# Rebuilding the opening of a fused two-layer adapter kernel: softmax, activation table, fillers, mixing matrices and column sums

## What is computed

```
y0 = grouped_conv1d(x, 9 taps, 4 groups) + (cond @ c_weight.T + side)      # layer 0
x1 = x + ffn0(y0)
h  = gelu(gelu(cond @ W0 + b0) @ W1 + b1);  att = softmax(h @ W2 + b2)     # 8 kernels, per sample
y1 = einsum('boi,bih->boh', att @ kernels, x1) + att @ bias_k              # layer 1
out = x1 + ffn1(y1)

ffn(y) = y @ W_base.T + b_base + 2 * sum_e gate_e(y) * (y @ A_e.T) @ B_e.T
gate   = softmax over the two largest of 8 logits y @ W_router.T, 0 elsewhere
```

## Time and profile before

| what | us |
|---|---|
| median of 3 runs | 398.42 |
| lowest and highest | 396.69, 398.55 |
| the profiled execution | 398.19 |
| its span, first to last instruction | 396.4 |
| TensorE busy | 386.1 |
| DVE, ScalarE, GpSimd busy | 280.5, 207.4, 226.6 |

### The profile page before, as it was taken

The page is one execution under the profiler, slowest core; times in us unless marked ns, Lnnn a source line. Parts: engine busy times, 40 slices in busy tenths (PEclk is TensorE's granted clock), DMA queues, the critical chain, the costliest instruction groups (busy, mean ns, idle before and its releaser), DMA issues.

```text
span 396.4 us, 9115 instructions
## 1 busy us (share of the span) xinstructions
PE 386.1 (97%) x2789; PEld 376.2 (95%) x2789; DVE 280.5 (71%) x983; ACT 207.4 (52%) x529; POOL 226.6 (57%) x199
## 2 busy tenths in 40 slices
PE   7989999999999999999999999999999999999996
PEld 6668999999999999999999999999999999999995
DVE  2787776767667776766777676677767667776764
ACT  3847455555445555544555554455555445555541
POOL 3387765555566565556656555665655566565560
PEclk9999999999999999999999999999999999999999
DMA  7871212222221122222111222212212221121101
GB/s 248 294 157 55 79 49 62 63 73 80 80 80 51 56 66 67 80 80 80 53 54 57 75 80 80 80 53 53 65 67 80 80 80 55 51 70 63 56 27 55
DMA packets 19821, 31.04 MB, mean 78 GB/s; under 512 B 5920, under 2 KB 6208, under 8 KB 19808
## 3 DMA queue, kind: packets, MB, share of 16 engines
q1 hardware_dynamic: 19808, 30.89, 25.2%
HBM read 21.97 MB, written 8.91 MB: 78 GB/s over the span
## 4 chain that ended last, share of the span: by engine, by line
PE 90%; DVE 4%; issue 2%; DMA 1%; ACT 1%; POOL 1%; SPq 0%; DVEq 0%; ACTq 0%; POOLq 0%
PE ps_out L336 33%; PE ps_out L348 22%; PE ps_out L368 11%; PE ps_conv L304 11%; PE ps_mix L384 5%; PE ps_t L316 4%; PE ps_mix L387 2%; DMA pack<-in_pack 1%; PE ps_t L355 1%; DVE yT L632 1%; PE ps_out L355 1%; DVE wb L632 1%; POOL x1b L902 1%; DVE lb_w L648 0%; PE ps_out L395 0%
## 5 line engine op out<-in xcount | busy, mean ns | idle before, releaser
L336 PE MATMUL ps_out<-wa,yT 128*128 128x392 f32 x768 | 152.4, 345 | 1.0 <-ACT yT L483 0.7
L336 PEld LDWEIGHTS ps_out<-wa,yT 128*128 128x128 f32 x768 | 132.2, 188 | 4.4 <-DVE yT L632 1.0
L889 POOL TENSOR_TENSOR x_part<-x,x_part 128x512 fp32r<-128x512 f32 x31 | 40.1, 1293 | 115.2 <-ACT x_part L483 115.2
L348 PE MATMUL ps_out<-wb,yT 128*128 128x256 f32 x768 | 104.4, 285 | 0.2 <-DVE wb L632 0.2
L348 PEld LDWEIGHTS ps_out<-wb,yT 128*128 128x128 f32 x768 | 96.0, 189 | 0.4 <-issue 0.4
L483 ACT ACTIVATE yT<-ps_t 64x256 fp32r<-64x256 f32 x128 | 48.4, 378 | 29.4 <-PE ps_t L316 26.9
L368 PE MATMUL ps_out<-lb_w,hwT 128*128 128x256 f32 x384 | 59.1, 289 | 1.1 <-issue 0.4
L632 DVE TENSOR_TENSOR yT<-ps_t,yT 64x256 fp32r<-64x256 f32 x128 | 53.8, 420 | 3.0
L902 POOL TENSOR_TENSOR x1b<-x,base_bias 128x512 f32<-128x512 f32 x30 | 39.7, 1324 | 26.4 <-DVE res L759 26.4
L520 ACT ACTIVATE wts<-top 128x1 f32<-128x1 f32 x128 | 30.3, 284 | 46.1 <-DVE top L723 46.1
L304 PE MATMUL ps_conv<-x_part,conv_w 128*128 128x256 f32 x384 | 52.1, 285 | 0.0
(11 more groups left out here) (93 smaller groups left out, 478.0 us busy)
## 6 DMA issues: line engine op xcount, KB each, us to landing
x_raw<-in_x_phase SPq DMA_DIRECT2D x32, 260.0 KB, 2.7
x_tok<-in_x_tok SPq DMA_DIRECT2D x32, 256.0 KB, 2.6
out<-res SPq DMA_DIRECT2D x31, 256.0 KB, 2.0
wa_raw<-in_wa SPq DMA_DIRECT2D x2, 784.0 KB, 8.1
wb_raw<-in_wb SPq DMA_DIRECT2D x2, 512.0 KB, 9.2
lb_raw<-in_lb SPq DMA_DIRECT2D x2, 256.0 KB, 6.1
bias<-in_bias SPq DMA_DIRECT2D x2, 256.0 KB, 6.0
scratch<-mix_nat SPq DMA_DIRECT2D x1, 512.0 KB, 2.8
```

The costliest lines, as they stand in the source:

```text
L336: last = mm(out_banks(y, t)[:, 0, 0:AR + DH], yT[y][dp][:, k, :], wa[y][:, wp, k, :], start=(n == 0 and k == 0), stop=(n == len(SPLITS) - ...
L348: last = mm(out_banks(y, t)[:, 1, OUT], yT[y][dp][:, k, :], wb[y][:, wp, k, :], start=(n == 0 and k == 0), stop=False, skip_group_check=True)
L889: g.tensor_tensor(x1_part[LO][:, :], x1[:, :], x1_part[HI][:, :].bitcast(F32), ALU.subtract).then_inc(s["x1l"], 1)
```

## The change

What it does, engine by engine:

- **Softmax.** `att` and `att_s` lie in PSUM, in free columns of `ps_mix`. exp(z) is taken as (1 + u)/(1 - u) = 2/(1 - u) - 1 with u = tanh(z/2), z the score less the maximum: ScalarE makes one tanh, DVE a subtraction with a halving, and then five small operations and the masked product.
- **Sigmoids.** In every routing, ScalarE makes half of the two top logits (`half_top`) and two tanh in place of two sigmoids; the gate adds 1 to them before it multiplies (one instruction, as before), and the factor of B is halved (`LORA`).
- **TensorE.** Nine fillers, conv 0 ahead of the small network, nine fillers before the turn of the probabilities in place of four. `mixing_setup` is issued inside tile 0's first product, ahead of its last four matmuls. Conv 2 is issued before step 1. The column sums are issued in step 1, behind `second_product(0, 1)`, into `ps_t0` and `ps_conv`.
- **Weights.** The high halves of wa are made in two parts, with a semaphore for each weight; ScalarE makes both copies of `mix_nat`, DVE none.
- **Tile 0's mixing matrix** is loaded straight from `mix_nat` in four small transfers, ahead of the way through DRAM, which carries tiles 1 to 31.
- **GpSimd** waits for the low half of B before it makes `xb` of tile 0; its sums for the column sums are spread between splits; x1b of tile 0 is made in another order (x1 and bias first, then `passed`).
- **SyncE** loads lb 0 and x 1 earlier, all weights of layer 1, then x 2 and x_tok 1, before it waits for `mix_nat`; x 3 and x_tok 2 follow the mixing transfers.
- Step 1 is written out on TensorE, ScalarE, DVE and GpSimd instead of being made by `step`.

The core of the diff; functions that only move are left out:

```diff
         ps_out = [ctx.enter_context(nc.psum_tensor(f"ps_out{y}", [P, 2, 512], F32)) for y in range(2)]
+        att = ps_mix[:, 1, ATT:ATT + 4 * E].rearrange("p (a e) -> p a e", e=E)
+        att_s = ps_mix[:, 1, ATT + 4 * E:ATT + 4 * E + 4]
         ps_hwT = [ps_out[0][:, 1, 0:P], ps_t0[:, 0:P]]
...
             load_x(0)
             sp.dma_start(pack[:, :], d["pack"]).then_inc(l_pack, 16)
             load_weights(0)
+            sp.dma_start(lb_raw[0][:, :], d["lb0"]).then_inc(l_lb[0], 16)
+            load_x(1)
             sp.dma_start(kern_sb[:, :], d["kern"]).then_inc(l_kern, 16)
             sp.dma_start(bk_sb[:, :], d["bk"]).then_inc(l_kern, 16)
-            sp.dma_start(lb_raw[0][:, :], d["lb0"]).then_inc(l_lb[0], 16)
+            load_tok(0)
             sp.dma_start(bias[0][:, :], d["bias0"]).then_inc(l_bias[0], 16)
-            load_tok(0)
-            load_x(1)
             load_weights(1)
-
+            sp.dma_start(lb_raw[1][:, :], d["lb1"]).then_inc(l_lb[1], 16)
+            sp.dma_start(bias[1][:, :], d["bias1"]).then_inc(l_bias[1], 16)
+            load_x(2)
+            load_tok(1)
+
+
+            sp.wait_ge(mix_zero, 1)
             sp.wait_ge(mix_nat_ready, 2)
+            for n in range(SPT):
+                sp.dma_start(mix[n * C:(n + 1) * C, n, :],
+                             mix_nat[n:n + 1, :].rearrange("p (i o) -> p i o", o=C)).then_inc(mix_first, 16)
             sp.dma_start(d["scratch"], mix_nat[:, :]).then_inc(mix_stored, 16)
-            load_x(2)
             sp.wait_ge(mix_stored, 16)
-            sp.wait_ge(mix_zero, 1)
             for j in range(SPT):
-                sp.dma_start(mix[j * C:(j + 1) * C, j::SPT, :],
-                             d["scratch"][j::SPT, :].rearrange("t (i o) -> i t o", o=C)).then_inc(mix_loaded, 16)
-            sp.dma_start(bias[1][:, :], d["bias1"]).then_inc(l_bias[1], 16)
-            load_tok(1)
-            sp.dma_start(lb_raw[1][:, :], d["lb1"]).then_inc(l_lb[1], 16)
+                sp.dma_start(mix[j * C:(j + 1) * C, SPT + j::SPT, :],
+                             d["scratch"][SPT + j::SPT, :].rearrange("t (i o) -> i t o", o=C)).then_inc(mix_loaded, 16)
 
...
@@ -319,15 +330,16 @@
             def first_product(y, t, before_low=None):
 
                 if isinstance(t, int) and t == 0:
-                    pe.wait_ge(w_hi[y], 1)
-                    pe.wait_ge(w_lo[y], 1)
+                    pe.wait_ge(wa_hi[y], 2)
                     if y == 1:
-                        pe.wait_ge(sums_ready, 2)
+                        pe.wait_ge(mix_nat_ready, 2)
 
                 if not (y == 1 and isinstance(t, int) and t == LAST):
                     need(pe, s["x1"] if y == 0 else s["out"], t)
                 pe.wait_ge(s["yh"][y], (t + 1) * YH[y])
                 for n, (dp, wp) in enumerate(SPLITS):
+                    if wp == LO and isinstance(t, int) and t == 0:
+                        pe.wait_ge(wa_lo[y], 2)
                     if dp == LO:
                         if before_low:
                             before_low()
...
                     mm(ps_out[0][:, 0, :], x1_part[HI][:, 0:P], x1_part[HI][:, :], start=True, stop=True)
 
-            keep_busy(10)
-
+            keep_busy(9)
+            conv(0)
             pe.wait_ge(l_pack, 16)
             mm(ps_mix[:, 1, 0:N], w0_sb, condT, start=True, stop=True).then_inc(mlp_mm, 1)
+            def column_sums_product():
+
+                pe.wait_ge(ones_ready, 1)
+                pe.wait_ge(k_summed, 3)
+                pe.wait_ge(s["y0"], 3)
+                pe.wait_ge(s["yl"][0], 2 * YL[0])
+                mm(ps_t0[:, 0:AR + DH], ones[:, :], k_sum[:, 0:AR + DH], start=True, stop=True)
+                mm(ps_conv[:, 0:DH], ones[:, :], k_sum[:, AR + DH:AR + D], start=True, stop=True).then_inc(sums_mm, 1)
 
             def step(t, has):
...
                 second_product(1, t - 1)
 
-            conv(0)
             kernel_scores()
             turn0(0)
-            keep_busy(4)
+            keep_busy(9)
             turn_probabilities()
             keep_busy(2)
-            mixing_setup()
-            first_product(0, 0)
+            first_product(0, 0, before_low=mixing_setup)
             conv(1)
             second_product(0, 0)
             turn_hw(0, 0)
             turn0(1)
             b_product(0, 0)
-
-            pe.wait_ge(ones_ready, 1)
-            pe.wait_ge(k_summed, 3)
-            pe.wait_ge(mix_nat_ready, 2)
-            mm(ps_out[1][:, 0, 0:AR + DH], ones[:, :], k_sum[:, 0:AR + DH], start=True, stop=True)
-            mm(ps_out[1][:, 1, OUT], ones[:, :], k_sum[:, AR + DH:AR + D], start=True, stop=True).then_inc(sums_mm, 1)
+            conv(2)
+
+            first_product(0, 1)
+            mix_product(0)
+            second_product(0, 1)
+            column_sums_product()
+            first_product(1, 0, before_low=lambda: turn_hw(0, 1))
+            pe.wait_ge(sums_ready, 2)
+            turn0(2)
+            b_product(0, 1)
+            second_product(1, 0)
             stages(pe, step)
 
             first_product(0, LAST)
...
+            def probabilities():
+
+                act.wait_ge(mlp_dve, 3)
+                nc.scalar.activation(att[:, 2, :], att[:, 1, :], ACT.Tanh).then_inc(mlp_act, 1)
+
+            def weigh(y, t):
+
+                act.wait_ge(s["top"][y], t + 1)
+                nc.scalar.activation(half_top[y][:, :], top[y][:, 0:2], ACT.Copy, scale=0.5).then_inc(s["half"][y], 1)
+                act.wait_ge(s["half"][y], t + 1)
+                for k in range(2):
+                    nc.scalar.activation(wts[y][:, k:k + 1], top[y][:, 1 - k:2 - k], ACT.Tanh, scale=-0.5,
+                                         bias=half_top[y][:, k:k + 1]).then_inc(s["wts"][y], 1)
...
+            high_wa_part(0, FIRST_KS)
+            probabilities()
+            high_wa_part(0, LAST_KS)
             turned0(0, 0)
             turned0(0, 1)
+            split_x(1)
             high_wb(0)
             high_lb(0)
-            split_x(1)
-            act.wait_ge(mixk_mm, 2)
-            copy(*mixing_half(1)).then_inc(mix_nat_ready, 1)
+            for q in range(2):
+                act.wait_ge(mixk_mm, q + 1)
+                copy(*mixing_half(q)).then_inc(mix_nat_ready, 1)
+            high_wa_part(1, FIRST_KS)
             weigh(0, 0)
-            high_wa(1)
+            high_wa_part(1, LAST_KS)
+            split_x(2)
             turned_hw(0, 0)
             turned0(1, 0)
             turned0(1, 1)
+            act.wait_ge(mix_first, 16 * SPT)
+            split_mix(0)
             split_x1(0)
+            high_wb(1)
+
+            weigh(0, 1)
+            save_cross(0)
+            turned1(0)
+            save_sums()
+            pass_bias(0)
             act.wait_ge(mix_loaded, 16 * SPT)
-            split_mix(0)
-            split_x(2)
+            split_mix(1)
+            split_x(3)
+            turned_hw(0, 1)
+            turned0(2, 0)
+            turned0(2, 1)
+            split_x1(1)
+            weigh(1, 0)
+            pass_bias(1)
+            high_lb(1)
...
+                v.tensor_reduce(att_s[:, 0:1], att[:, 0, :], AX.X, ALU.max).then_inc(mlp_dve, 1)
+                dve.wait_ge(mlp_dve, 2)
+                v.tensor_scalar(att[:, 1, :], att[:, 0, :], att_s[:, 0:1], 0.5, ALU.subtract,
+                                ALU.mult).then_inc(mlp_dve, 1)
 
             def probabilities():
 
                 dve.wait_ge(mlp_act, 3)
+                v.tensor_scalar(att[:, 1, :], att[:, 2, :], -1.0, 1.0, ALU.mult, ALU.add).then_inc(mlp_dve, 1)
+                dve.wait_ge(mlp_dve, 4)
+                v.reciprocal(att[:, 3, :], att[:, 1, :]).then_inc(mlp_dve, 1)
+                dve.wait_ge(mlp_dve, 5)
+                v.tensor_scalar(att[:, 0, :], att[:, 3, :], 2.0, -1.0, ALU.mult, ALU.add).then_inc(mlp_dve, 1)
+                dve.wait_ge(mlp_dve, 6)
+                v.tensor_reduce(att_s[:, 1:2], att[:, 0, :], AX.X, ALU.add).then_inc(mlp_dve, 1)
+                dve.wait_ge(mlp_dve, 7)
                 v.reciprocal(att_s[:, 2:3], att_s[:, 1:2]).then_inc(mlp_dve, 1)
-                dve.wait_ge(mlp_dve, 3)
-                v.scalar_tensor_tensor(out=att_m[:, :, :], in0=att[:, 1:2, :].to_broadcast([P, SPT, E]),
+                dve.wait_ge(mlp_dve, 8)
+                v.scalar_tensor_tensor(out=att_m[:, :, :], in0=att[:, 0:1, :].to_broadcast([P, SPT, E]),
                                        scalar=att_s[:, 2:3], in1=own.rearrange("p (j e) -> p j e", e=E), op0=ALU.mult,
                                        op1=ALU.mult).then_inc(mlp_dve, 1)
...
-                link(v.tensor_tensor(pairs(y, t, WEIGHED), pairs(y, t, EQUAL),
-                                     wts[y][:, :].unsqueeze(2).to_broadcast([P, 2, E]), ALU.mult))
+                link(v.scalar_tensor_tensor(out=pairs(y, t, WEIGHED), in0=wts[y][:, :].unsqueeze(2).to_broadcast([P, 2, E]),
```

(50 more changed lines are left out.)

110 lines of the change are left out of this document (50 added, 60 removed).

## The result

The changed kernel takes 392.95 us (median of 4 runs, 392.74 to 393.21), the kernel before, measured beside it, 398.49 us (median of 4, 396.69 to 400.1). The ratio is 0.9876, 95% interval 0.9849 to 0.9903. The profiled execution took 393.21 us, with a span of 391.4; before, it had a span of 396.4. The 5.0 us are explained from these two traces.

A forecast was written before the change was run, and what follows sets the result against it. TensorE, busy 97% of the span, was taken as the bound, so gains came only before 51.84 us: -2.35 (opening) - 0.35 (clock) + 0.3 (end) = -2.4 us on 398.19, forecast 395.8 us, range 393.7 to 398.0.

The forecast's parts named there:

- Clock at the start: Opening matmuls of the kernel before: TensorE at 1.2 GHz, rising to 2.4 GHz after an unbroken stretch of conv work.
- Clock: TensorE from 1.46 to 9.6 us: an early rise gains 0.75 us, a late one costs 0.6; -0.35 us taken.
- Softmax in PSUM: Opening, scores to turned probabilities: 0.21 us a link, turn at 13.8 us; the 1.0 us gain spent on the longer chain.
- One activation table: ScalarE's table loads before the exp and the sigmoids: both already hidden, their removal costed at nothing.
- a table is still loaded: Rival, softmax: tanh not living with gelu leaves a 1.28 us load, costing 0.95 us; 396.75 us, chance 0.1.
- Mixing matrices inside the first product: Tile 0's first product on TensorE: starts at 14.4 us, mixing products fill its wait, gain 0.7 us.
- Second product of tile 0: After conv 1: wb's low half ends near 17.6 us, the product starts at 20.0 without a wait, gain 1.1 us.
- Tile 0's end: Third factor: DVE's wa stands behind POOL's split of x, TensorE idles 1.6 us; mixing product at 27.8 instead of 30.40.
- Column sums: Step 1 on TensorE: a 0.9 us wait for POOL until 31.1 us; tile 2's first product at 37.2 instead of 39.60.
- Queues: Tile 0's small mixing transfers: leave at 19.9 to 21.3 us; 3.6 us or less costs nothing, 6 us costs 1.4.
- Every step and the end: Routing delayed 0.3 us by an extra ScalarE instruction: covered in steady steps, +0.3 us at the very end.
- more is gained: Rival, opening: the clock rises early and one meeting of POOL and DVE does not happen; 394.3 us, chance 0.14.

The follow-up runs named there:

- after_old_layout: The changed kernel with every SBUF buffer at the address it had before the change, no instruction differing: 394.99 us, ratio 0.9943, step 11.540 us.
- before_new_layout: The kernel before with every SBUF buffer at its address in the changed kernel, no instruction differing: 396.23 us, ratio 0.996, step 11.493 us.
- after_yt_160_lower: The changed kernel with yT alone another 160 bytes lower (-320 from its old place, modulo 2048): 391.99 us, ratio 0.9843, step 11.440 us.
- after_exp_softmax: The changed kernel with the old softmax (exp in SBUF), the routing keeping its tanh: 394.52 us, ratio 0.9919.
- after_yt_320_lower: The changed kernel with yT alone another 320 bytes lower (-480 from its old place, modulo 2048): 395.67 us, ratio 0.9943, step 11.567 us.
- after_mixed_layout: The changed kernel with unused SBUF bytes, 160 ahead of x_raw and 1888 behind x_part: 393.63 us, ratio 0.9895, step 11.498 us.
- after_again: The changed kernel itself measured once more, nothing changed: 393.25 us, ratio 0.9886, step 11.489 us.
- before_conv0_first: The kernel before with nine fillers instead of ten and conv 0 ahead of the small network: 398.19 us, ratio 1.0045.
- after_mixing_outside: The changed kernel with the mixing products ahead of tile 0's first product, as before: 394.44 us, ratio 0.9913.
- after_4_fillers: The changed kernel with four fillers instead of nine ahead of the turn of the probabilities: 393.31 us, ratio 0.9891.

## Why the prediction missed

**"A step costs its matmuls, and the change adds or removes no matmul in them. So a gain can only come from the stretch before 51.84 us."** This failed, and with 1.55 us it is the larger part of the 2.6 us by which the forecast missed the profiled span (-2.4 against -5.0). The matmuls are the same in number and shape, but not in time: their operands stand at other places. after_old_layout and before_new_layout show it from both sides. Steps of 11.54 us were among the signs I named; the sign I called wrong was only the longer one.

**"Clock at the start" and "Clock".** The clock rose inside the unbroken stretch, as the larger case had it. I had taken half of 0.75 us. Conv 0 ended at 7.31 instead of 7.9, the small network ran at 2.4 GHz, and the scores' product came at 9.00 instead of 10.3. There was some luck in it: the small network also waits for the landing of `pack`, which the sum left out. In after_yt_160_lower the clock rose earlier, at 5.2 us, but TensorE waited 0.71 us for `pack`, and the scores' product came at 9.65.

**"Softmax in PSUM."** A link is one small instruction that waits for the one before. Taken at 0.26 us a link, the links measured 0.21 to 0.25 (first 9.43, 9.64, 9.85, then 10.88 to 11.96 behind the tanh). The turn came at 12.27 instead of 13.8: 1.3 us by the earlier scores' product, 0.2 by the links. "The gain of 1.0 us is spent on the longer chain" was wrong by that much: the chain is 0.3 us longer than the exp's in the same order (after_exp_softmax), which is what the links cost.

**"One activation table", costed at nothing.** Wrong as a statement on the new order: there the load costs 0.6 to 0.9 us in front of the sigmoids, and 1.07 us of TensorE's wait behind the exp. Both were hidden in the old order, as the earlier trace rows said. In the new order what hid them was gone, and I costed a removal by its cover of before. In the sum it made no difference, since the new order was added up without loads. The rival *a table is still loaded* is out: one load, at the start.

**"Mixing matrices inside the first product"** and **"Second product of tile 0".** Their order came as forecast: the eight high matmuls, the mixing products, the last four, conv 1, and the second product without a wait, all of it 1.2 to 1.5 us early with the turn. The gain of 0.7 us for the mixing products was too small: with them ahead of the first product, tile 3's first product is 1.45 us later, and the time 0.8 us or more longer even with the clock up.

**"Tile 0's end": the wait of 1.6 us did not come.** VectorE's low half of wa started first and POOL's split stood behind it, not the other way round. The timeline of the two:

```profile
19.89 0.96 DVE L677 TENSOR_TENSOR wa<-wa_raw,wa 128x784 fp32r<-128x784 f32 x1
```

```profile
19.92 2.10 POOL L939 TENSOR_TENSOR x_part<-x_raw,x_part 128x520 fp32r<-128x520 f32 x1 [1.71 <-ACT x_part L507]
...
27.95 1.56 POOL L996 TENSOR_TENSOR k_sum<-k_sums 128x648 f32<-128x648 f32 x1
```

A difference of 0.03 us decides who stands. The rule of the port held (POOL's split took 2.10 us instead of 1.3); who comes first could not be had from sums that are 1 us off. Tile 1's first product started at 23.38, 2.3 us ahead of the forecast, 1.1 of it from this.

**"Column sums."** Right: POOL's last sum ends at 29.5, TensorE waits 1.01 us where I had 0.9. This wait took part of the gain back: the mixing product was 1.8 us ahead of the forecast, the column sums 1.5, tile 2's first product (35.74 against 37.2) 1.5.

**"Step 2."** It took 48.21 - 35.74 = 12.5 us, where the addition had 12.7.

**"Queues", "Every step and the end."** The small transfers left at 18.7 and landed at 23.7 (3.07 us for the last); the mixing product waited 0.25. No routing held a steady step. The end is 0.18 us longer, 0.3 forecast; the sigmoids in its place gave 0.23 back.

So the forecast of -2.70 us up to tile 3 was -3.63: 0.4 of the rest is the half of the clock term I left out, the other 0.5 the shorter links and the meeting on the port that did not happen, less what the column sums took back; these were not separated by a run. The rival *more is gained* described the opening well (its two conditions both came true), and its 394.3 us less the 1.55 us of the steps, which no case of mine held, is 392.75, near the 392.95 measured.

## What to carry over

Before a step is called untouched, compare the addresses of its buffers: a kernel that TensorE bounds to 98% moved by 1% when one operand was put 160 bytes away (-320 to -480 in the table), so an edit that adds or drops a small buffer is also a change of layout, and a pad is a cheap thing to try last. A cost hidden in the old order must be looked at again in the new one: what hid the two table loads went away with the change. Where the sum hangs on who takes a shared port first, by less than the sum's own error, the case with the other order belongs in the range.

## What the runs showed that was not expected

- The place of one matmul operand in SBUF changes the time of the second products by up to 6% (1.36 to 1.44 us for twelve matmuls) and the step between 11.440 and 11.567 us with the other buffers as in the changed kernel, between 11.511 and 11.599 with them as before. Two places 1024 bytes apart are alike (11.489 and 11.487).
- The moment of the clock's first rise differs from run to run of one order. By the spacing of the matmuls it came at 11.0 us in the profile of the kernel before, and near 5.1 with the same order and other places. In the profiles of the changed kernel and its variants it lies between 4.4 us (after_yt_320_lower) and 7.6 (after_mixed_layout). The changed kernel itself had conv 0 in 1.84 us (after) and 2.42 us (after_again), and tile 3's first product at 48.21 and 48.48. The granted clock of the profile reads 1.00 all through that stretch.
- The clock fell to 0.50 for some 3 us from 15 or 16 us on in three of the sixteen profiles (before_conv0_first, before_new_layout, after_mixing_outside), the third without a long idle time ahead of it, and did not in after_4_fillers with TensorE some two thirds idle for 2 us, nor in after_exp_softmax with its wait of 1.07 us.
